# Keys of heads 2 and 3, maxima in halves and narrow column sums in a two-layer graph attention kernel

## The reference

```
fea = x^T;  W = adj * A(mean over channels)            # 1024 x 1024, A from a sigmoid of differences
g   = relu((fea @ W) * para);  q = g^T                 # 4 heads of 64 channels
k, v = split(x @ kv_w)
out = softmax(q k^T * scale) v   for each of 4 heads;  x = layernorm(x + out)
```

## Time and profile before

| what | us |
|---|---|
| median of 3 runs (2951.5 to 2953.19) | 2952.94 |
| the profiled execution | 2955.18 |
| its span, first to last instruction | 2953.4 |
| PE busy (share of the span) | 2784.0 (94%) |
| DVE busy | 1921.6 (65%) |
| ACT busy | 1671.3 (57%) |
| POOL busy | 1286.9 (44%) |

### The profile page before, as it was taken

How to read it: one execution, slowest core, us unless ns; L and a number is a source line. 1 busy time by engine, 2 the same in 40 slices (tenths; PEclk the granted TensorE clock), 3 DMA queues, 4 the chain that set the end, 5 groups by cost and what they waited for, 6 DMA issues and landing times. The chain is left out here.

```text
span 2953.4 us, 39152 instructions
## 1 busy us (share of the span) xinstructions
PE 2784.0 (94%) x12308; PEld 1872.3 (63%) x12308; DVE 1921.6 (65%) x2821; ACT 1671.3 (57%) x2148; POOL 1286.9 (44%) x700
## 2 busy tenths in 40 slices
PE   7999999999999999999999999997799999989954
PEld 5565665656656565665656656563588888868843
DVE  5677776876768677786776768674533333348877
ACT  6566575766667666575665667653422222237767
POOL 3755657565475755657565475745200000000024
PEclk9999999999999999999999999999799999999976
DMA  4123222232222223222232222220332223205547
GB/s 136 58 79 104 75 71 72 71 103 85 65 75 78 71 82 100 75 71 74 68 103 85 64 75 78 71 74 25 117 114 86 85 99 114 85 29 186 183 173 283
DMA packets 125646, 276.20 MB, mean 94 GB/s; under 512 B 12192, under 2 KB 62368, under 8 KB 119456
## 3 DMA queue, kind: packets, MB, share of 16 engines
q1 hardware_dynamic: 125600, 275.62, 29.0%
HBM read 178.79 MB, written 62.98 MB: 82 GB/s over the span
## 5 line engine op out<-in xcount | busy, mean ns | idle before, releaser
L302 POOL TENSOR_TENSOR psum<-psum,probs 128x1024 f32<-128x1024 f32 x320 | 790.5, 2470 | 188.9 <-ACT probs L370 169.7
L370 ACT ACTIVATE probs<-sc_ps 128x1024 f32<-128x1024 f32 x512 | 503.0, 1023 | 430.8 <-PE sc_ps L816 404.3
L542 DVE TENSOR_REDUCE mx<-mx_ps 128x1 f32<-128x512 f32 x768 | 494.6, 686 | 369.2 <-PE mx_ps L784 362.8
L832 PE MATMUL pv_ps<-probs,v 128*64 128x512 f32 x2048 | 489.9, 602 | 0.0
L816 PE MATMUL sc_ps<-qa,ka 128*128 128x512 f32 x1024 | 381.2, 403 | 0.0
L816 PE MATMUL sc_ps<-qb,kb 128*128 128x512 f32 x1024 | 372.6, 394 | 0.5
L784 PE MATMUL mx_ps<-ka,qa 128*128 128x512 f32 x768 | 284.3, 428 | 10.6 <-DVE mx L542 8.9
L832 PEld LDWEIGHTS pv_ps<-probs,v 128*64 128x64 f32 x2048 | 129.9, 136 | 225.8 <-issue 196.9
L816 PEld LDWEIGHTS sc_ps<-qa,ka 128*128 128x128 f32 x1024 | 187.4, 188 | 111.8 <-issue 64.1
L784 PEld LDWEIGHTS mx_ps<-ka,qa 128*128 128x128 f32 x768 | 133.8, 187 | 189.7 <-DVE mx L542 108.2
L1175 DVE TENSOR_TENSOR agg_lo<-ag_ps,agg_hi 128x1024 fp32r<-128x1024 f32 x32 | 39.2, 1225 | 313.6 <-ACT agg_hi L1102 313.6
(11 more groups left out here) (180 smaller groups left out, 5475.6 us busy)
## 6 DMA issues: line engine op xcount, KB each, us to landing
adj_ring<-in_adj_dram SPq DMA_DIRECT2D x128, 512.0 KB, 3.7
pre_scratch<-pre SPq DMA_DIRECT2D x28, 1024.0 KB, 4.7
pre<-pre_scratch SPq DMA_DIRECT2D x28, 1024.0 KB, 4.9
x<-in_x_dram SPq DMA_DIRECT2D x16, 1024.0 KB, 5.7
kb<-ka SPq DMA_DIRECT2D x64, 256.0 KB, 3.3
qa<-qa SPq DMA_DIRECT2D x64, 256.0 KB, 3.1
res<-in_x_dram SPq DMA_DIRECT2D x16, 1024.0 KB, 5.7
x_scratch<-res SPq DMA_DIRECT2D x16, 1024.0 KB, 4.5
```

The lines of the kernel that those rows point to most:

```text
L302: pool.tensor_tensor(psum[:, h % 2, :], probs[:, 0, :] if k == 1 else psum[:, h % 2, :], probs[:, k % PR, :], ALU.add).then_inc(s["pool_ad ...
L370: nc.scalar.activation(probs[:, i % PR, :], sc_ps[:, t % 2, :], ACT.Exp, scale=SCALE)\
L542: nc.vector.tensor_reduce(mx2[:, nh, n:n + 1], mx_ps[:, nh, :], AX.X, ALU.max)\
L832: ins = nc.tensor.matmul(pv_ps[nh * HD:(nh + 1) * HD, h % 2, :], v[:, i, h * HD:(h + 1) * HD], probs[:, i % PR, nh * BANK:(nh + 1) * BANK] ...
```

## The change

1. `k_piece` goes. `k_product` gets a second call, `k_product(b, 1)`, which makes the keys of heads 2 and 3 in `mx_ps` after tile n = 3 of g. `k_high` for them moves in front of `q_high` on ACT, and `k_low` moves in front of `row_stats` on DVE, out of the maxima of head 0.
2. The order after g: one tile of values, maxima tiles 0 and 1, then values and maxima in turn; all values stand before `transpose_maxima`. On ACT `v_copy(b, 0)` moves ahead of `relu_q(b, 1)`, and x of the next batch is rounded in parts of 6 and 2 tiles.
3. The maxima of the next head are placed by halves, up to one or two before each step of the scores, and two halves for head 1 stand before the part of head 0 that waits for the row.
4. `sum_up` uses 32 columns of ones and four products of 256 columns, one to each column group of 32. So `den_copy` copies 256 columns instead of 512, and `transpose_sums` makes 2 transposes instead of 4.

```diff
+    MAX_HALVES = [[[2, 1, 1], [1, 1, 1, 1, 0], [2, 1, 1, 1, 1], [1, 1, 0, 0, 0]]] + \
+        2 * [[[0, 1, 1, 1, 1], [1, 1, 1, 1, 0], [2, 1, 1, 1, 1], [1, 1, 0, 0, 0]]]
...
-        ones = sb("ones_a", [P, HD])
+        ones = sb("ones_a", [P, SG])
...
     (ACT, after w_high(b, 7))
+                k_high(b, 2)
+                k_high(b, 3)
                 q_high(b, 0)
                 q_high(b, 1)
                 relu_q(b, 0)
                 q_high(b, 2)
                 q_high(b, 3)
-                k_high(b, 2)
-                k_high(b, 3)
+                v_copy(b, 0)
                 relu_q(b, 1)
                 if not last:
-                    x_high(b + 1, range(0, 4))
-                v_copy(b, 0)
+                    x_high(b + 1, range(0, 6))
+                v_copy(b, 1)
                 if not last:
-                    x_high(b + 1, range(4, T))
-                v_copy(b, 1)
+                    x_high(b + 1, range(6, T))
...
     (DVE, after w_low(b, 7))
+                k_low(b, 2)
+                k_low(b, 3)
                 if before:
                     row_stats(b - 1)
...
-                maxima(b, 0, range(0, 4))
-                k_low(b, 2)
-                maxima(b, 0, range(4, 5))
-                k_low(b, 3)
-                maxima(b, 0, range(5, T))
+                maxima(b, 0, range(T))
...
     (PE, g_product)
                     if before and n == 3:
                         transpose_back(b - 1, HEADS - 1)
+                    if n == 3:
+                        k_product(b, 1)
...
     (PE, sum_up; SG = 32, SN = 256)
-                for nh in range(NH):
-                    ins = nc.tensor.matmul(pv_ps[nh * HD:(nh + 1) * HD, h % 2, :], ones[:, :],
-                                           psum[:, h % 2, nh * BANK:(nh + 1) * BANK], start=True, stop=True)
+                for g in range(4):
+                    ins = nc.tensor.matmul(pv_ps[g * SG:(g + 1) * SG, h % 2, 0:SN], ones[:, :],
+                                           psum[:, h % 2, g * SN:(g + 1) * SN], start=True, stop=True)
...
     (PE, transpose_sums; SQ = 2)
-                for q in range(4):
+                for q in range(SQ):
...
     (PE, body)
                 g_product(b)
-                k_piece(b, 0, 0)
-                k_piece(b, 0, 1)
+                v_product(b, 0, [0])
                 max_scores(b, 0, 0)
                 max_scores(b, 0, 1)
-                k_piece(b, 1, 0)
-                max_scores(b, 0, 2)
-                k_piece(b, 1, 1)
-                max_scores(b, 0, 3)
-                for m in range(4):
+                for m in range(1, 4):
                     v_product(b, 0, [m])
-                    max_scores(b, 0, 4 + m)
-                v_product(b, 1, [0, 1])
+                    max_scores(b, 0, m + 1)
+                max_scores(b, 0, 5)
+                v_product(b, 1, [0])
+                max_scores(b, 0, 6)
+                v_product(b, 1, [1])
+                max_scores(b, 0, 7)
+                v_product(b, 1, [2, 3])
                 transpose_maxima(b, 0)
-
-                v_product(b, 1, [2, 3])
...
                     for p in range(PAIRS):
                         i = 2 * p
                         if p == 0:
+                            units = [(n, [0], range(NH)) for n in (i, i + 1) if h]
+                            units += [(n, [1], range(NH)) for n in (i, i + 1)]
                         else:
+                            units = [(n, (0, 1), [nh]) for n in (i, i + 1) for nh in range(NH)]
+                        for k, (n, parts, part_halves) in enumerate(units):
+                            maxes(p, k)
+                            scores(b, h, n, parts, part_halves)
+                        maxes(p, len(units))
```

More of the change, by code:

```diff
@@ L340, in k_high @@
                 wait(act, s["k_ready"], 2 * b + h // 2 + 1)
-                src = (mx_ps, pv_ps)[h // 2]
-                nc.scalar.activation(ka[h][own(h), :], src[own(h), :, :].rearrange("p a n -> p (a n)"), ACT.Copy)\
+                nc.scalar.activation(ka[h][own(h), :], mx_ps[own(h), :, :].rearrange("p a n -> p (a n)"), ACT.Copy)\
                     .then_inc(s["kh_done"], 1)
@@ L383, in den_copy @@
                 wait(act, s["back_ready"], 4 * b + h)
[L384 removed]
+                nc.scalar.activation(heads_t[:, (h + 1) % 2, 0:SN], pv_ps[:, h % 2, 0:SN], ACT.Copy)\
                     .then_inc(s["den_copied"], 1)
@@ L519, in k_low @@
                 wait(dve, s["kh_done"], 4 * b + h + 1)
-                src = (mx_ps, pv_ps)[h // 2]
-                nc.vector.tensor_tensor(ka[h][other(h), :], src[own(h), :, :].rearrange("p a n -> p (a n)"),
+                nc.vector.tensor_tensor(ka[h][other(h), :], mx_ps[own(h), :, :].rearrange("p a n -> p (a n)"),
                                         ka[h][own(h), :].bitcast(F32), ALU.subtract).then_inc(s["kl_done"], 1)
@@ L703, in k_terms, with k_product @@
                                     for k in range(CT)])
-            def k_product(b):
-                wait(pe, s["xtl_done"], 2 * b + 2)
-                wait(pe, s["row_done"], 4 * b)
+            def k_product(b, c):
+                if c == 0:
+                    wait(pe, s["xtl_done"], 2 * b + 2)
+                    wait(pe, s["row_done"], 4 * b)
+                else:
+                    wait(pe, s["kl_done"], 4 * b + 2)
                 for nh in range(NH):
-                    ins = product(mx_ps[:, nh, :], k_terms(0, nh))
+                    ins = product(mx_ps[:, nh, :], k_terms(c, nh))
                 ins.then_inc(s["k_ready"], 1)
[L712 to L720, removed]
             def v_product(b, j, tiles=range(4)):
                 if j == 0:
-                    wait(pe, s["kl_done"], 4 * b + 2)
+                    wait(pe, s["kl_done"], 4 * b + 4)
                 else:
@@ L771, in max_scores @@
                         wait(pe, s["max_done"], 64 * b + 2 * (n - 1))
-                elif n == 0:
+                elif n == 0 and 0 in halves:
                     wait(pe, s["row_done"], 4 * b + h)
@@ L777, in max_scores @@
                         wait(pe, s["v_evac"], 2 * b + 2)
-                for nh in range(NH):
+                for nh in halves:
                     if h and n:
@@ L793, in transpose_maxima, with scores @@
                 nc.tensor.transpose(out, mxs[:, :], ident[:, :]).then_inc(s["rowT_ready"], 1)
-            def scores(b, h, i, parts=(0, 1)):
+            def scores(b, h, i, parts=(0, 1), halves=range(NH)):
                 t = 8 * h + i
-                if 0 in parts:
+                if 0 in parts and 0 in halves:
                     wait(pe, s["exp_done"], 32 * b + t - 1)
@@ L806, in scores @@
                         wait(pe, s["kl_done"], 4 * b + h + 1)
-                if 1 in parts and i == 0:
+                if 1 in parts and 0 in halves and i == 0:
                     wait(pe, s["row_in"], 16 * (4 * b + h + 1))
@@ L817, in scores @@
                                                start=part == 0, stop=part == 1)
-                if 1 in parts:
+                if 1 in parts and NH - 1 in halves:
                     ins.then_inc(s["st_ready"], 1)
@@ L825, in values @@
                 wait(pe, s["exp_done"], 32 * b + t + 1)
-                if i == 0 and h < 2:
+                if i == 0:
                     wait(pe, s["v_evac"], 2 * b + 2)
-                    wait(pe, s["kl_done"], 4 * b + 4)
-                elif i == 0:
                     wait(pe, s["res_added"], 4 * b + h - 1)
@@ L891, in body, with maxes @@
                     more = h + 1 < HEADS
[L892 to L896, removed]
+                    halves = iter(range(NH * T))
+                    def maxes(p, k):
+                        for j in itertools.islice(halves, MAX_HALVES[h][p][k] if more else 0):
+                            max_scores(b, h + 1, j // NH, [j % NH])
                     for p in range(PAIRS):
                         i = 2 * p
-                        maxes(MAX_FIRST[p])
                         if p == 0:
[L902 to L907, removed]
-                        else:
[L909 to L912, removed]
+                            units = [(n, [0], range(NH)) for n in (i, i + 1) if h]
+                            units += [(n, [1], range(NH)) for n in (i, i + 1)]
+                        else:
+                            units = [(n, (0, 1), [nh]) for n in (i, i + 1) for nh in range(NH)]
[3 more added lines that the diff above has]
+                        maxes(p, len(units))
                         if h and p == DEN_PAIR:
```

17 lines of the change are left out of this document (8 added, 9 removed).

## The result

The changed kernel takes 3061.07 us (median of 4 runs, 3048.81 to 3062.45), the kernel before 2952.22 us. The ratio is 1.0356, with a 95% interval of 1.0334 to 1.0378: 3.6% slower, where about 1% faster was forecast. The profiled execution is the 3048.81 one.

The account below looks back on a forecast made before the run. PE, busy 94% of the span, was taken as the bound. Per batch -0.04 + 0.15 - 0.56 - 0.84 - 0.65 = -1.94 us, x 16 = -31, first batch -1.5 more: 2952.9 - 32.5 = about 2921 us, range 2898 to 2943.

Parts of the forecast that it names:

- its first: Opening step, all of layer 0: PE bounds the kernel, clock slices at 9 (2.4 GHz), so no term depends on the clock.
- narrow products that take turns: Rival, column sums: 32-column groups aren't overlapped, 1.95 us instead of 0.6, +86 us, 3007 us; chance 0.07.
- The late DVE: Start of head 0's maxima: g waits 1.5 us for DVE, maxima start 2.8 us after g, PE stands 2.1 us.
- Stage g,: Stage g: keys +2.74, narrow sum -0.43, two fewer transposes -0.22, in all +2.09 us per batch.
- POOL's additions holding up `add_last`: Sign of being wrong: these additions delay `add_last` and by it the maxima of head 2; no size given.
- Maxima and row: Head 0: first maxima to transpose 11.25 us instead of 13.06; pair 1 starts 4.1 us after the transpose.
- The move pays for itself: Moved keys: stage g's +2.09 against -2.13 us from end of g to pair 1, nothing gained or lost.
- Heads: Heads, per batch: small waits +0.15, single halves -0.56, three sums -0.84, three pairs of transposes -0.65 us.
- DVE not late: Rival, ahead of head 0's maxima: the 1.5 us stall doesn't come up, 23 us less, 2898 us; chance 0.12.

Follow-up runs that it names:

- 0.87 us: Changed kernel with 8 spare matmuls of 512 columns after the first tile of values, DVE as late as before: 2948.82 us, 0.9983 of before.
- 1.79: Changed kernel with 4 spare matmuls of 512 columns after the first tile of values: 3025.18 us, 1.0265 of before.
- 2.52: Kernel before, with 9 spare statistics instructions on DVE ahead of `q_times_para(b, 0)`: 3096.81 us, 1.0484 of before.
- the keys alone: Kernel before with only the keys moved and their order of values, ACT and DVE, row statistics ahead of `w_low(b, 7)`: 2963.1 us, 1.0028 of before.
- with the halves: Changed kernel, row statistics ahead of `w_low(b, 7)`, `weigh` behind `k_low`: 2901.08 us; compared with the kernel before plus narrow sums, halves and that `weigh` order: 2910.56 us.
- the statistics forward: Changed kernel with `row_stats` and `moments` on DVE before `w_low(b, 7)` instead of after `k_low(b, 3)`; PE's wait 0.70 us: 2917.75 us, 0.9881 of before.

## Why the prediction was wrong, step by step

The step that failed is its first: "the clock slices are at 9, ... so no term depends on the clock". That row says what the clock did under the idle times of the kernel before, in whose middle batches no two starts on PE are more than 1.1 us apart. The prediction then forecast an idle of 2.1 us and priced it at its length. It had to ask what a gap of a length that no middle batch shows does to the clock. The runs, by the gap ahead of the first maxima: 0.70 and 0.87 us, no fall in 14 batches each, both with 1.45 us ahead of the last sum as well; 1.79, 9 falls; 2.52 to 2.61, 12 to 14. A fall costs 7 to 9 us, three times the gap itself, and in all 112 us. A row on it was at hand in the trace of before, hidden in the first of the slices at 9: its granted clock fell for 6.8 us in the first batch, at 35.4 us, at the end of a gap of 5.66 us between two matmuls of g (PE's timeline, then that stretch):

```profile
30.91 0.39 PE L748 MATMUL sc_ps<-w_lo,x_hi 128*128 128x512 f32 x1
36.57 0.79 PE L748 MATMUL sc_ps<-w_hi,x_hi 128*128 128x512 f32 x1 [5.28 <-DVE w_lo L515]
```

```profile
35.40:42.20 6.80, 5.63 (x13) 4.46 (x14) 6.05 (x6) 6.35 (x7) 0.00 (x0) 0.50 0.52 157
```

It would have warned of a fall, not of its price: twice the gap, and the clock was back three times as soon as behind the gaps ahead of the maxima. None of the rivals had the clock in it; the one that ended slower, narrow products that take turns, was wrong.

- *The late DVE.* Right in kind, place and nearly in size, as the changed kernel's rows show. ACT waits for PE ahead of `w_high(b, 7)`, DVE for ACT, and `q_times_para` starts without idle time (ACT's timeline, then DVE's, then PE's, of the second batch):

```profile
172.42 1.06 ACT L339 ACTIVATE w_hi<-scr 128x1024 fp32r<-128x1024 f32 x1 [3.60 <-PE sc_ps L739]
```

```profile
173.51 1.23 DVE L516 TENSOR_TENSOR w_lo<-scr,w_hi 128x1024 fp32r<-128x1024 f32 x1 [2.43 <-ACT w_hi L339]
174.77 2.47 DVE L521 TENSOR_TENSOR ka<-mx_ps,ka 64x1024 fp32r<-64x1024 f32 x2
177.27 2.71 DVE L584 BATCH_NORM_STATS2 stats<-res 128x6 f32<-128x256 f32 x8
...
181.07 2.35 DVE L529 TENSOR_TENSOR scr<-sc_ps,neg_para 128x1024 f32<-128x1024 f32 x2
```

```profile
180.32 0.28 PE L677 MATMUL mx_ps<-kvw_hi,xT_hi 128*128 128x256 f32 x1
...
183.52 1.19 PE L775 MATMUL sc_ps<-ka,qa 64*128 64x512 f32 x4 [2.33 <-DVE scr L529]
```

  Before, `q_times_para` started 1.16 us ahead of the end of g, now 0.75 behind it: 1.9 us late, where 1.5 were forecast. The idle is 2.6 instead of 2.1 us.
- *Stage g,* forecast +2.09, measured +3.21. The keys (+2.72), the sum (0.57 us for 1.01) and the transposes (-0.22) are as forecast. What is missing is a wait of 1.1 us more ahead of the sum, from DVE's collision with POOL. This is the second step that failed: the sum gives every product of g its own length and no wait, though less work for PE in the heads leaves DVE, which has as much as before, 0.5 us later against it. "POOL's additions holding up `add_last`" stood among the signs of being wrong, but with no price in the sum and at another place.
- *Maxima and row.* The maxima are right: 11.11 us for 11.25. The row isn't: the scores of pair 1 start 4.73 us after the transpose, not 4.1. PE's timeline of the changed kernel, whose transpose starts at 194.63:

```profile
195.56 1.17 PE L806 MATMUL sc_ps<-qa,ka 128*128 128x512 f32 x4 [0.67 <-DVE row L553]
196.57 0.62 PE L775 MATMUL mx_ps<-ka,qa 128*128 128x512 f32 x2
197.28 0.70 PE L806 MATMUL sc_ps<-qb,kb 128*128 128x512 f32 x2
197.82 0.42 PE L775 MATMUL mx_ps<-ka,qa 128*128 128x512 f32 x1
198.07 0.62 PE L806 MATMUL sc_ps<-qb,kb 128*128 128x512 f32 x2
198.53 0.99 PE L775 MATMUL mx_ps<-ka,qa 128*128 128x512 f32 x2
199.36 0.41 PE L806 MATMUL sc_ps<-qa,ka 128*128 128x512 f32 x1
```

  The second part of the scores does start when forecast, 2.65 us after the transpose. But behind it the sum counts two halves and the kernel has three before pair 1, and the third starts 0.48 us after the one before it (both are in the 0.99 us row), where 0.23 is its plain length. That makes 1.03 us saved instead of 1.67 (5.77 - 4.1).
- *The move pays for itself.* It didn't. By the forecast, from the start of g to pair 1 nothing changes (-0.04); measured, with the clock kept, it is +3.21 + 1.75 - 1.94 - 1.03 = +2.0 us, 1.1 of them the wait for the last sum. The +0.6 us of the keys alone and the -0.4 with the halves were measured with the statistics forward, that is without the late DVE, and don't bear the forecast out.
- *Heads.* Nearly right: from the transpose to the next g -3.22 us, forecast -3.57; the 0.64 us missing at the row are half made up for behind it. The new change of shape from 32 to 64 columns is paid, but less than the 0.15 us taken for it: a sum takes 0.57 us from its start to the values, where 0.63 was forecast with it and 0.48 without, so 0.09. The rule of the Trainium skill (TensorEngine Tiling (Array Packing), Key Properties), that a change of tiling mode drains the engine, agrees with that. Three sums so save 3 x 0.34 us and the transposes 0.65, together 1.67; that only 1.50 of it arrives, just what was forecast, is luck, and where the other 0.17 goes no row was read for. The narrow sums, one in a head and one in g, PE's timeline of the changed kernel:

```profile
221.85 0.64 PE L830 MATMUL pv_ps<-psum,ones_a 128*32 128x256 f32 x8
222.42 1.94 PE L820 MATMUL pv_ps<-probs,v 128*64 128x512 f32 x8
...
284.70 0.64 PE L830 MATMUL pv_ps<-psum,ones_a 128*32 128x256 f32 x8 [1.06 <-DVE psum L559]
285.27 0.50 PE L739 MATMUL sc_ps<-w_hi,x_hi 128*128 128x512 f32 x1
```

  All eight records fit into 0.57 us: the four column groups run together.
- *DVE not late* as a rival: it became true only by the reordering, and then at 2918 us, 31 below the kernel that keeps its clock.

## What to carry to other kernels

Before a change that opens a gap on PE, compare its length with the longest gap behind which the trace shows an unchanged clock. Beyond that, the price can be the gap and a stretch of matmuls at half speed, and here a gap of 2.61 us instead of 0.70 turned a gain of 1.2% into a loss of 3.6%. And when a step gets faster, look which pairs of DVE and POOL instructions lie within a few tenths of a microsecond of each other: here their order decided whether DVE took 1.2 us or 3.4.

## What the hardware showed that was not expected

- A gap of 2.5 to 2.6 us in PE's starts is followed, -0.4 to 2.5 us after the work resumes, by 17.1 to 23.9 us at 1.2 GHz. It needn't happen each time: in the profiled execution of the changed kernel batches 1 and 2 had the same gap of 2.61 us and kept the clock, and with 1.79 us 5 of 14 did. The other executions took 12 to 14 us more than the profiled one (3060.8 to 3062.45 us), as much as two more falls would take; their mean clock is 0.928 to 0.930 for 0.936.
- Where the gap is 2.61 us, every batch behind the first fall falls too. With 1.79 us it isn't so: batches 1 and 2 fell, 3 to 5 kept the clock, 6 fell again. What decides in which batch the clock falls isn't shown.
- A longer gap isn't a longer fall. Behind the 5.66 us within g, in the first batch, the clock was back after 3.4 to 6.8 us in all twelve traces; behind 1.79 to 2.61 us ahead of the maxima it took 17.1 to 23.9. Products of 128 rows and 512 columns follow the first, 64-row maxima in turn with other products and waits the second. No run puts the one gap ahead of the other work, so the reason is open.
- Four column groups of 32 start 7 ns after one another, all within 20 ns, and the second pass of 256 columns in fp32 starts 0.24 us after the first, half of the 0.48 of 512 columns in two groups. The changes of shape at both ends come to 0.1 us beside that.
- `weigh` on DVE, with both operands in SBUF, takes 1.2 us when it starts ahead of POOL's addition, and 1.2 and about what the addition has left when it starts within it: 3.4 us with 2.3 left, 1.6 with 0.6 left. `k_low`, with one operand in PSUM, took 1.22 us beside POOL's addition in the kernel before (2.48 for two).
